# Four fused convolution blocks: the last 3x3 convolution on pairs of rows of one image

## The reference

```python
x = x + L0(gn(x))   # layer norm, super-token attention
x = x + L1(gn(x))   # routed grouped 3x3 convolution
x = x + L2(gn(x))   # depthwise convolutions, deformable sampling, scan
x = x + L3(gn(x))
# L3(v):
m3 = (j - i) % 4 == 0          # i: output channel, j: input channel
out = conv3x3(v, w3 * m3)      # padding 1
out = out + einsum('oi,bihw->bohw', w1 * ~m3, v)
out = out + b.sum(axis=1)
```

## Time and profile before

| | us |
|---|---|
| median of 3 runs (2990.2 to 2994.64) | 2993.04 |
| the profiled execution | 2988.49 |
| its span | 2986.7 |

### The profile page before, as it was taken

How to read it: one execution, slowest core, us unless ns; L and a number is a source line. 1 busy time by engine, 2 the same in 40 slices (tenths; PEclk the granted TensorE clock), 3 DMA queues, 4 the chain that set the end, 5 groups by cost and what they waited for, 6 DMA issues and landing times.

```text
span 2986.7 us, 33573 instructions
## 1 busy us (share of the span) xinstructions
PE 2469.6 (83%) x8551; PEld 1293.2 (43%) x8551; DVE 2075.6 (69%) x3325; ACT 1376.0 (46%) x2100; POOL 1159.6 (39%) x965
## 2 busy tenths in 40 slices
PE   4896769699968888869968967778899688888799
PEld 2595535334433333324426954443344333333243
DVE  5544746498858998976655447456987588989665
ACT  3632533567745555551035236226676355555400
POOL 2200027360037777743311000455400477777332
PEclk9898989899979999989978988889999799999899
DMA  4000459200000000001210006590000000000011
GB/s 153 1 1 1 149 195 175 42 1 0 1 0 1 0 0 0 0 1 77 106 43 1 0 0 224 144 184 9 1 1 1 1 1 0 0 0 0 7 49 56
DMA packets 60866, 121.29 MB, mean 41 GB/s; under 512 B 2487, under 2 KB 39999, under 8 KB 56407
## 3 DMA queue, kind: packets, MB, share of 16 engines
q1 hardware_dynamic: 60759, 120.04, 14.6%
HBM read 64.65 MB, written 55.38 MB: 40 GB/s over the span
## 4 chain that ended last, share of the span: by engine, by line
PE 58%; DVE 18%; issue 9%; ACT 5%; DMA 4%; POOL 3%; DVEq 2%; ACTq 0%; SPq 0%; POOLq 0%
PE PSUM L638 11%; PE PSUM L1808 9%; PE PSUM L1986 6%; PE PSUM L922 4%; POOL BIG L831 3%; DVE BIG L757 3%; PE PSUM L1851 2%; DVE BIG L733 2%; PE PSUM L2044 2%; PE PSUM L2038 2%; PE PSUM L1865 2%; PE PSUM L2026 2%; PE PSUM L916 2%; PE PSUM L1868 2%; PE PSUM L2000 2%
## 5 line engine op out<-in xcount | busy, mean ns | idle before, releaser
L733 DVE TENSOR_TENSOR BIG<-PSUM,BIG 128x512 f32<-128x512 f32 x576 | 383.5, 684 | 100.8 <-POOL BIG L831 30.3
L982 DVE SCALAR_TENSOR_TENSOR PSUM<-BIG,VECS,PSUM 128x1024 f32<-128x1024 f32 x272 | 350.3, 1288 | 111.7 <-PE PSUM L1808 105.4
L831 POOL TENSOR_TENSOR BIG<-BIG 128x512 f32<-128x512 f32 x256 | 345.9, 1351 | 147.5 <-DVE BIG L780 129.5
L638 PE MATMUL PSUM<-BIG,WL 128*128 128x512 f32 x768 | 335.1, 599 | 14.8 <-POOL BIG L621 14.8
L671 POOL TENSOR_TENSOR BIG<-TOEP,BIG 128x384 f32<-128x384 f32 x84 | 97.1, 1182 | 609.9 <-DVE BIG L1371 609.9
L1808 PE MATMUL PSUM<-BIG,WDW 128*128 128x512 f32 x704 | 317.4, 601 | 9.0 <-ACT BIG L1740 9.0
L916 PE MATMUL PSUM<-BIG,SELB 120*128 120x512 bf16 x576 | 224.5, 392 | 120.1 <-DVE BIG L733 116.0
L922 PE MATMUL PSUM<-BIG,CSTS 128*128 128x512 f32 x512 | 270.5, 610 | 0.0
L638 PEld LDWEIGHTS PSUM<-BIG,WL 128*128 128x128 f32 x768 | 147.7, 193 | 200.8 <-issue 200.8
L812 POOL TENSOR_TENSOR BIG<-BIG 128x96 f32<-128x96 f32 x192 | 68.9, 384 | 382.2 <-ACT BIG L873 382.2
L916 PEld LDWEIGHTS PSUM<-BIG,SELB 120*128 120x128 bf16 x576 | 56.0, 97 | 345.8 <-DVE BIG L733 298.0
(11 more groups left out here) (327 smaller groups left out, 5140.8 us busy)
## 6 DMA issues: line engine op xcount, KB each, us to landing
spill<-X SPq DMA_DIRECT2D x18, 1024.0 KB, 5.8
back_spill<-BIG SPq DMA_DIRECT2D x32, 576.0 KB, 7.2
X<-x SPq DMA_DIRECT2D x8, 2048.0 KB, 10.5
out<-BIG SPq DMA_DIRECT2D x32, 512.0 KB, 2.6
X<-back_spill SPq DMA_DIRECT2D x16, 1008.0 KB, 14.7
BIG<-fc SPq DMA_DIRECT2D x8, 1024.0 KB, 9.7
BIG<-rt_spill SPq DMA_DIRECT2D x2, 832.0 KB, 8.0
rt_spill<-BIG SPq DMA_DIRECT2D x1, 832.0 KB, 3.4
```

Source lines behind the costliest of these rows:

```text
L638: ins = pe.matmul(PSUM[:, 4 * k + m, :].rearrange("p (r j) -> p r j", r=8), w[:, dy, m, :], VC[:, k, m, dy:dy + 8, :], start=(dy == 0), st ...
L733: dve.tensor_tensor(img(o), img(PSUM[:, (k + q) % 2, :]), pch(c, XBASE, dy, dx), ALU.mult).then_inc(df_p, 1)
L831: pool.tensor_tensor(XS[:, k, :], XS[:, k, :], PRD[:, product_buffer(q), :], ALU.add).then_inc(df_add, 1)
L982: return dve.scalar_tensor_tensor(out=rows8(to), in0=strip(c, base, dy, dx), scalar=vc(weights, j), in1=rows8(acc), op0=ALU.mult, op1=ALU.add)
```

## The change

L3 works on one image at a time, and the 128 partitions of its input are the 64 channels of an odd row and the 64 channels of the even row after it. The 128 outputs are two rows of that image. The three row offsets then fall into two products instead of three, with weights that have three of four 64 x 64 blocks filled.

- `pair_rows` (SP) copies `X` into the new layout `RAW3` (65 pairs of rows of each image, 130 columns a row) by 16 DMAs in 8 parts of 16 pairs of rows. Part n waits until part n-2 has landed; the outputs come behind all 8 parts in SP's list. `RAW3` lies where `PAD` lay. An output strip is now 16 rows of one image, written by two DMAs (even rows, odd rows). A strip of the next `X` is loaded behind each output strip instead of a quarter behind each four; the first load is in strips too.
- ACT normalises `RAW3` in place, in 16 pieces, three strips ahead, and adds the first product and the bias out of PSUM into `OBUF` (`add_columns_act`). DVE adds the other four terms.
- The residual is no longer added by DVE. It goes through the centre weight: `residual` (DVE) adds 0.5/scale or -0.5/scale on the diagonal of the two middle weights, and the channel's mean goes into the bias. Four small products on PE spread scale and shift over both halves of the partitions.
- `columns_pe` takes m in the order 0, 3, 1, 2: first POOL's, then DVE's. All loops of the stage are unrolled.
- The set-up builds the new weights on DVE: two memsets and 19 small copies more, the other operations half as wide.

```diff
         VC = r.take(2, 4, 9 * (W // 2)) ...
+        RAW3 = BIG[:, 0:2 * ODD * PW].rearrange("p (s j w) -> p s j w", s=2, j=ODD)
@@ sync
+                def pair_rows(n):
+
+                    if n >= 2:
+                        sp.wait_ge(moved[n % 2], parts_moved(pair, n - 2))
+                        settle(sp)
+                    q, i = n // 4, n % 4
+                    a = 16 * i + 1
+                    sp.dma_start(RAW3[0:C, q, a:a + 16, 1:1 + W],
+                                 X[q * C:(q + 1) * C, 2 * a - 1:2 * a + 30:2, :]).then_inc(moved[n % 2], 16)
+                    lo, hi = (0 if i == 0 else a), min(a + 16, H // 2)
+                    sp.dma_start(RAW3[C:P, q, lo:hi, 1:1 + W],
+                                 X[q * C:(q + 1) * C, 2 * lo:2 * hi - 1:2, :]).then_inc(moved[n % 2], 16)
...
+                for n in (PARTS3 - 2, PARTS3 - 1):
+                    sp.wait_ge(moved[n % 2], parts_moved(pair, n))
...
+                for S in range(NS):
+                    q, t, k = S // 8, S % 8, S % 2
+                    sp.wait_ge(cv_done, pair * NS + (S + 1 + CREDIT))
...
+                    for h in range(2):
+                        sp.dma_start(out[bass.ds(pair * P + q * C, C), 16 * t + h:16 * t + 15 + h:2, :],
+                                     OBUF[h * C:(h + 1) * C, k, :].rearrange("p (r w) -> p r w", r=8)).then_inc(out_dma[k], 16)
                     with sp.If(pair < PAIRS - 1):
-                        load_quarter(j, ...
+                        load_strip(S, ...
@@ the helpers of the stage
+        def columns_pe(pe, pair, S):
+            q, k = S // 8, S % 2
+            if S >= 2:
+                pe.wait_ge(cv_done, pair * NS + (S - 1 + CREDIT))
+            for m in (0, 3, 1, 2):
...
+                for b in range(2):
+                    w = WL3[:, b, m // 3, :] if m in (0, 3) else WMID[:, q, b, m - 1, :]
+                    ins = pe.matmul(PSUM[:, 4 * k + m, :].rearrange("p (r j) -> p r j", r=8), w,
+                                    VC[:, k, m, b:b + 8, :], start=(b == 0), stop=(b == 1))
+            ins.then_inc(cv_mm, 1)
...
+        def add_columns_act(act, pair, S):
+            m, to = column_sums(S), halves(S % 2)
+            act.wait_ge(cv_mm, pair * NS + (S + 1 + CREDIT))
+            act.wait_ge(out_dma[S % 2], pair * (NS * 16) + (S // 2 + 1) * 32)
+            settle(act)
+            for e in range(2):
+                ins = act.activation(to[e], m[e], ACT.Identity, bias=BIAS3[:, S // 8:S // 8 + 1])
+            ins.then_inc(from_psum, 1)
@@ vector
+                residual(0)
+                columns_dve(dve, pair_l3, 0)
+                residual(1)
+                for S in range(NS):
+                    if S + 1 < NS:
+                        columns_dve(dve, pair_l3, S + 1)
+                    add_columns_dve(dve, pair_l3, S)
@@ scalar
+                for S in range(3):
+                    normed_rows(S)
+                for S in range(NS):
+                    if S + 3 < NS:
+                        normed_rows(S + 3)
+                    add_columns_act(act, pair, S)
```

More of the change, by code:

```diff
@@ L74 @@
 NREG = 11560
+ODD = H // 2 + 1
 WINDOWS, WROW, WCH = 9, 16, 8
@@ L83 @@
 BACK = (UNITS // 2 + 2) * 16
+PARTS3 = 8
+SPREAD = [(WINDOWS + 1 - k) // 2 * 16 for k in range(2)]
+MOVES = [n + PARTS3 * 16 for n in SPREAD]
 EXPT = EXPERTS * 8 * 36
@@ L586, in far_pe, with columns @@
             settle(pe)
[L592 to L596, removed]
+        def columns(S):
+            q, t = S // 8, S % 8
+            d0, d1 = (RAW3[:, q, 8 * t:8 * t + 9, 0:W].rearrange("p r (j e) -> p e r j", e=2)[:, e] for e in range(2))
+            d2, d3 = (RAW3[:, q, 8 * t:8 * t + 9, 2:W + 2].rearrange("p r (j e) -> p e r j", e=2)[:, e] for e in range(2))
@@ L597, in columns, with columns_dve @@
             return d0, d1, d2, d3
[L599 to L611, removed]
+        def columns_dve(dve, pair, S):
+            k = S % 2
+            d0, d1, d2, d3 = columns(S)
+            dve.wait_ge(l3_xn, pair * NS + (S + 1))
+            if S >= 2:
+                dve.wait_ge(cv_mm, pair * NS + (S - 1 + CREDIT))
@@ L612, in columns_dve @@
             dve.tensor_tensor(VC[:, k, 1], d1, d2, ALU.add)
             dve.tensor_tensor(VC[:, k, 2], d2, d1, ALU.subtract).then_inc(cv_vector, 1)
[L615 to L640, removed]
@@ L642, in halves, with columns_pool @@
-        def halves(a):
-            v = a.rearrange("p r (j e) -> p e r j", e=2)
-            return v[:, 0], v[:, 1]
[L647 to L659, removed]
+        def columns_pool(pool, pair, S):
+            k = S % 2
+            d0, d1, d2, d3 = columns(S)
+            pool.wait_ge(l3_xn, pair * NS + (S + 1))
+            if S >= 2:
+                pool.wait_ge(cv_mm, pair * NS + (S - 1 + CREDIT))
+            settle(pool)
+            pool.tensor_tensor(VC[:, k, 0], d0, d2, ALU.subtract)
+            pool.tensor_tensor(VC[:, k, 3], d1, d3, ALU.subtract).then_inc(cv_pool, 1)
@@ new lines, in halves, with column_sums @@
+        def halves(k):
+            v = OBUF[:, k, :].rearrange("p (r j e) -> p e r j", r=8, e=2)
+            return v[:, 0], v[:, 1]
+        def column_sums(S):
+            return [PSUM[:, 4 * (S % 2) + m, :].rearrange("p (r j) -> p r j", r=8) for m in range(4)]
+        def add_columns_act(act, pair, S):
[6 more added lines that the diff above has]
+            ins.then_inc(from_psum, 1)
@@ new lines, in _, with residual @@
+                dve.tensor_scalar(BIAS3, NORM3[:, :, 3], SM[:, 8:9], None, ALU.add).then_inc(fold_bias, 1)
+                dve.wait_ge(fold_bias, pair_l3 * 3 + 3)
+                dve.wait_ge(border, pair_l3 * 3 + 4)
+                settle(dve)
+                def residual(q):
+                    for b, rows, cols in ((0, slice(C, P), slice(0, C)), (1, slice(0, C), slice(C, P))):
+                        for m in range(2):
+                            ins = dve.scalar_tensor_tensor(out=WMID[rows, q, b, m, cols], in0=ident[rows, rows],
+                                                           scalar=HALF3[rows, m, q:q + 1], in1=WCROSS[rows, m, :],
+                                                           op0=ALU.mult, op1=ALU.add)
+                    ins.then_inc(fold_w, 1)
@@ L1764, in _, with normed_rows, rows @@
                 group_norm(pair * 4 + 3)
-                act.wait_ge(border, pair * 3 + 4)
-                settle(act)
-                with act.Fori(0, NT) as t:
-                    normed(t, pch(t), l3_xn)
+                act.wait_ge(l1_mom, pair * 16 + 16)
+                act.wait_ge(fold_bias, pair * 3 + 3)
+                def normed_rows(S):
+                    q, t = S // 8, S % 8
+                    act.wait_ge(moved[S // 2 % 2], parts_moved(pair, S // 2))
+                    settle(act)
+                    def rows(lo, hi, j0, j1):
+                        a = RAW3[lo:hi, q, j0:j1, 1:1 + W]
+                        return act.activation(a, a, ACT.Identity, bias=NORM3[lo:hi, q, 0:1], scale=NORM3[lo:hi, q, 1:2])
+                    if t == 0:
+                        rows(C, P, 0, 1)
+                    if t == 7:
+                        rows(0, C, ODD - 1, ODD)
+                    rows(0, P, 8 * t + 1, min(8 * t + 9, ODD - 1)).then_inc(l3_xn, 1)
+                for S in range(3):
+                    normed_rows(S)
+                for S in range(NS):
+                    if S + 3 < NS:
+                        normed_rows(S + 3)
+                    add_columns_act(act, pair, S)
         @block.tensor
@@ L2058, in _ @@
                 group_norm(pair * 4 + 3)
-                columns_pe(pe, pair, WL3)
+                pe.wait_ge(l1_mom, pair * 16 + 15)
+                for q in range(2):
+                    for h in range(2):
+                        ins = pe.matmul(PSUM[h * C:(h + 1) * C, 7, 8 + 4 * q:12 + 4 * q], ident[:, q * C:(q + 1) * C],
+                                        SM[:, 4:8], start=True, stop=True)
+                ins.then_inc(l1_bc_pe, 1)
+                pe.wait_ge(l1_mom, pair * 16 + 16)
+                for S in range(NS):
+                    columns_pe(pe, pair, S)
 def constants():
```

162 lines of the change are left out of this document (97 added, 65 removed).

## The result

| | before | after |
|---|---|---|
| median, us | 2993.84 (4 runs, 2990.2 to 2996.69) | 2920.03 (4 runs, 2915.11 to 2928.06) |
| the profiled execution, us | 2988.49 | 2928.06 |
| its span, us | 2986.7 | 2926.2 |

The ratio is 0.9759, with a 95% interval from 0.9741 to 0.9776: the change takes off 74 us by the medians (72 by the ratio), and 2913 was forecast.

The account below looks back on a forecast made before the run. PE was taken to bound the stage. Stages 42.0 and 42.4 us shorter, less 2.3 set-up and 1.7 end, give 80.4 off 2988.5, so 2908.1; with 4.6 to the median, 2912.6 us, range 2886 to 2958.

Parts of the forecast that it names:

- PE's work: PE products of L3: 16 instructions a strip instead of 24, 6.87 us instead of 10.30, 55 us less for each pair.
- The copies' rate: SP's copies of X into RAW3: 200 GB/s between 64 partitions, 41.9 us, all landed at T0 + 43.3.
- Two parts are in flight, so the waits inside cost nothing: SP's copies into RAW3: with two parts of 5 us each in flight, waits between parts add 0 us.
- What waits for the copies: Outputs behind all copies on SP: strip 4 starts 8.3 us after them, PE idles 9.6, stage ends 97.1 after them.
- Start of the stage: Group norm, first copy part, ACT and POOL before PE's first product: PE starts at T0 + 12.0, 0.9 us later.
- What hides the rest: Steady strips of L3: DVE needs 4.9 us of PE's 6.87, POOL 3.4, ACT 1.1 + 1.2, so PE never waits.
- Set-up: DVE's weight building ahead of the statistics: larger memset, 19 more copies and a wait, wide operations halved; 2.3 us more.
- End: Last output of the kernel, two DMAs of 64 partitions: 4.3 us instead of 2.6, so 1.7 more.
- Rival A: Copies into RAW3 run at 286 GB/s, PE never idles before strip 4, stage 128.3 us, total 2888 us; chance 0.15.
- Rival B: Unaligned RAW3 rows slow the copies to 133 GB/s, stage 161.6 us, total 2956 us; chance 0.2.
- Rival C: Narrow ends and short rows add up in the copies: 82 GB/s, stage 200.8 us, total 3036 us; chance 0.1.
- D: Gain eaten elsewhere, by outputs falling behind or instruction loads for unrolled code: time within 0.2% of before; chance 0.05.

Follow-up runs that it names:

- the last experiment: Against the version with outputs 0 to 3 between the last copies: first copy part split, L3's set-up weights built later on DVE; median 2883.16 us.
- the first experiment: Against the changed kernel: outputs of strips 0 to 3 issued between the last copies, next X loads from strip 4 on; median 2887.41 us.

## Why the prediction was right

The median is 7 us above the forecast, well inside the range, and the mechanism is the forecast one: sixteen copies ahead of the outputs, one gap of PE in front of strip 4, half clock behind it. Some of the nearness of the number is luck, as the sum below shows. Point by point, by its own steps:

- **PE's work: right.** 256 instructions in each stage, 592 ns each at the full clock as the trace models them, issued every 0.429 us: eight take 3.43 from start to start (L667 at 1349.79 and at 1353.22). The fuller weights leave the clock at 1.00.
- **The copies' rate: the mis-sized term.** The step said "I take the middle, 200 GB/s". The trace has 187 to 188 in the windows, and over the whole 8.39 MB / (48.8 - 1.3) us = 177, lower in the later parts (179 from 1348 to 1377). The first output came at T0 + 48.9 instead of 43.3. That is +5.6 for each pair. With the 2.3 us of fixed part that the run with one part in flight gives, 1.0 of the 5.6 is the fixed part and 4.6 the rate, then 180 GB/s. The rule of the Trainium skill named there ("SBUF — State Buffer", 196 GB/s) gave 44.2, nearer by 0.9 only.
- **"Two parts are in flight, so the waits inside cost nothing": near.** Taking one away costs 14.8 us, 2.1 for each of the seven waits. That two are enough for the full rate was not tested with three.
- **What waits for the copies: right in mechanism and size.** Copies to strip 4: 8.5 us for 8.3. Copies to the end of the stage: 96.9 and 98.3 for 97.1. The half clock behind the gap costs 2.0 in the first pair and 3.3 in the second (the time of 192 instructions less 82.4) for 2.5. The gap was 12.8 and 13.2 for 9.6.
- **Start of the stage: one term missed, and hidden.** The numbers were ready at T0 + 6.35 (7.2 forecast), but the first part landed at T0 + 8.5, not "just before" at 6.7, and PE started at T0 + 13.8 instead of 12.0. The second part behind it in the queue is not the reason, since with one part in flight the first landed at T0 + 8.5 too; the larger fixed part and the lower rate make 1.4 of the 1.8 us. It cost nothing here because of the gap behind it. Once the gap is gone it counts: the last experiment takes it away and each stage is 2.7 us shorter (128.2 against 130.9).
- **What hides the rest: right.** No gap on PE behind strip 4, DVE at 54% of the steady part. "Taking the residual off DVE gains nothing by itself" was not tested alone; that the first sum on ACT gains nothing was.
- **Set-up +2.3: measured +2.5** (34.75 against 32.21). **End +1.7: +1.8** (5.1 from the last sum to the end of the span, 3.3 before).
- **The sum.** In the profiled executions: stages 36.6 and 35.7 shorter, set-up and end 4.3 longer, and 7.5 us more in stretches that the change does not touch (3.5 ahead of the first T0, 4.0 between the stages). These do the same work as before. They vary from run to run: the stretch between the stages is 1294.8 us before, 1298.8 in the change, 1292.3 in the first experiment, 1291.4 in that with 32 partitions. So they are no cost of the change as far as these runs tell. Stages, set-up and end alone come to a gain of 68.0, where 80.4 was forecast; most of the 12.4 between are the copies, twice 5.6. The medians lie 73.8 apart, so some 6 us of the nearness come from stretches that the prediction did not speak of.
- **Rival A (286 GB/s)** is what copies on 128 partitions give: stages of 128.3 and 128.1 for 128.3 forecast, 2886.72 for 2888. **Rival B (unaligned rows cost a third of the rate)** fell: 188 against 191 with aligned ones. The Trainium skill's account of how a row off the 256-byte boundaries takes more transactions ("DMA: Bandwidth & Descriptors", "How a descriptor splits into AXI transactions") may be what the busy share shows, but no time hangs on it in these copies. The prediction's 133 took every transaction to cost the same, which the section does not say. **Rival C (82 GB/s)** fell with the rate, **D** with the time and the steady part.

What stays open: whether the source or the destination holds the copies at 187 GB/s, since both ends are narrow in every run but that on 128 partitions. Nearest to it are the outputs, 64 partitions to DRAM, with the halves in turn: the first two strips of the second pair run at 233 GB/s (2825.8 to 2827.8). That speaks against the source alone, but does not settle it. Not tried: more than two parts in flight, starting the copies ahead of the last rows of `X` (`RAW3` lies over buffers that L2 still reads), and hiding the 19 us of statistics between the pairs in DVE's slack.

## What to carry to other kernels

A rearrangement by DMA costs little when the stage has other work to cover it; what costs is work that stands behind it in the same queue. Ask of each DMA queue what is issued behind a bulk transfer and how many buffers the consumers have until it leaves: here the same copies, with four outputs moved between them, gave back 31 us in the two stages. And once one gap is closed, look at the start again: a late first piece that the gap had hidden is then on the path.

## What the runs showed of the hardware

- SBUF to SBUF in rows of 512 bytes: 187 to 188 GB/s between 64 partitions and 64, 185 between 32 and 32, 285 between 128 and 128. Alternating the halves gave 180.
- The busy share of the DMA engines was 1.20, and 1.26 with 32 partitions, when the destination's rows did not start on multiples of 512 bytes, and 0.92 when they did, at nearly the same rate (188, 185 and 191 GB/s). What a share above 1 means is not shown here; it did not tell how much rate was left.
- With one part of 1.05 MB in flight instead of two, a part took 7.95 us (133 GB/s from 1335 to 1390): 14.8 us more over seven waits, 2.1 for each.
- PE came back from 13 us of idle time below its full clock, at a cost of 2.0 us in the first stage and 3.3 in the second (granted clock 0.50 from 1377.4 to 1379.4, within the gap, and 0.62 in the 4.7 us behind it).
